# An adaptive-layernorm block on one core: another order in the prologue, the last unit and the end, and other slots for the feed-forward rows

## What is computed

```python
mod = (silu(c) @ wmod).reshape(2, 6, 1, 512)        # sa, ca, ga, sb, cb, gb
ga, gb = sign(g) * max(|g|, 0.25)                   # for both gates
h = layernorm(x) * (1 + ca) + sa
q, k, v = rope(h @ wq), rope(h @ wk), h @ wv
att = softmax(causal(q @ k.T / sqrt(128)))
x = x + ga * ((att @ v) @ wo)
h = layernorm(x) * (1 + cb) + sb
x1, x2 = split(h @ w12.T + b12)
out = x + gb * ((silu(x1) * x2) @ w3.T + b3)
```

## Time and profile before

| | us |
|---|---|
| median of three runs | 795.87 |
| the profiled execution | 795.66 |
| its span, first to last instruction | 793.9 |
| PE busy in it | 765.9 (96%) |
| DVE busy | 604.0 (76%) |
| POOL busy | 567.8 (72%) |
| ACT busy | 507.3 (64%) |

### The profile page before, as it was taken

One profiled execution on the slowest core, in us unless ns is written; L12 is line 12 of the kernel. 1 busy time (PEld: TensorE's weight loads), 2 busy tenths in 40 slices (PEclk: granted clock), 3 DMA queues, 4 the chain that ended last, 5 costly groups with the idle time before them and its releaser, 6 DMA issues.

```text
span 793.9 us, 11522 instructions
## 1 busy us (share of the span) xinstructions
PE 765.9 (96%) x3526; PEld 623.4 (79%) x3526; DVE 604.0 (76%) x1296; ACT 507.3 (64%) x1201; POOL 567.8 (72%) x384
## 2 busy tenths in 40 slices
PE   7999999999999999999999999999999998889997
PEld 2755788887888788887888888888888877667885
DVE  5777878777877787778778786868787788459685
ACT  2466775776676766786677666767677765865331
POOL 2545885879587957795779677898768998447453
PEclk9999999999999999999999999999999999999999
DMA  9625646874867576867776767866677855989011
GB/s 314 232 66 143 204 132 186 193 248 117 238 154 234 157 218 154 219 185 199 182 212 190 192 186 189 251 158 211 145 228 188 280 146 170 272 264 248 1 54 53
DMA packets 189781, 147.13 MB, mean 185 GB/s; under 512 B 60564, under 2 KB 166164, under 8 KB 187672
## 3 DMA queue, kind: packets, MB, share of 16 engines
q1 hardware_dynamic: 189304, 146.33, 65.1%
q10 hardware_dynamic: 416, 0.07, 0.0%
HBM read 91.82 MB, written 54.53 MB: 184 GB/s over the span
## 4 chain that ended last, share of the span: by engine, by line
PE 50%; POOL 22%; DVE 11%; ACT 10%; issue 4%; DMA 3%; SPq 1%; DVEq 0%; ACTq 0%; POOLq 0%
PE q_bank L511 12%; PE out_bank L599 11%; POOL pT_lo L1412 7%; PE o_bank L576 7%; PE x_bank L511 7%; PE s_bank L511 5%; POOL rope_tmp L1438 4%; ACT probs L1185 3%; POOL qT L1412 3%; POOL wo_lo_sb L1412 3%; ACT probs L1193 2%; POOL wq_lo_sb L1412 2%; PE s_bank L798 1%; PE s_bank L785 1%; DVE x_y L1134 1%
## 5 line engine op out<-in xcount | busy, mean ns | idle before, releaser
L1412 POOL TENSOR_TENSOR pT_lo<-pT_raw,pT_hi 128x1024 fp32r<-128x1024 f32 (+1 forms) x96 | 194.2, 2038 | 60.1 <-ACT pT_hi L1162 60.1
L1185 ACT ACTIVATE probs<-probs,neg_max 128x32 f32<-128x32 f32 (+15 forms) x256 | 130.6, 512 | 144.8 <-DVE neg_max L860 144.8
L1412 POOL TENSOR_TENSOR qT<-rope_tmp,qT 128x512 fp32r<-128x512 f32 x64 | 83.7, 1308 | 85.4 <-ACT qT L1162 85.4
L878 DVE STREAM_TRANSPOSE turned<-probs 128x512 f32<-128x512 f32 (+1 forms) x64 | 96.7, 1511 | 36.3 <-DMA spread_dram<-turned 28.3
L1438 POOL TENSOR_TENSOR rope_tmp<-rope_tmp 128x512 f32<-128x512 f32 x80 | 110.4, 1388 | 13.2 <-DVE rope_tmp L825 9.4
L1193 ACT ACTIVATE probs<-probs,row_inv 128x32 f32<-128x32 f32 (+15 forms) x256 | 111.9, 508 | 1.8 <-DVE row_inv L868 1.8
L511 PE MATMUL s_bank<-k_both,qT 128*128 128x416 f32 (+11 forms) x576 | 100.6, 324 | 2.0 <-DVE neg_max L860 2.0
L511 PE MATMUL q_bank<-hT_hi,wq_hi_sb 128*128 128x512 f32 x244 | 97.2, 399 | 5.1 <-DVE rope_tmp L825 5.1
L860 DVE CUSTOM_DVE_ANT_0 probs<-s_bank,mask_sb 128x416 f32<-128x416 f32 (+2 forms) x192 | 87.0, 501 | 15.9 <-PE s_bank L511 15.7
L511 PEld LDWEIGHTS s_bank<-k_both,qT 128*128 128x128 f32 x576 | 90.4, 191 | 9.9 <-DVE neg_max L860 2.6
L599 PE MATMUL out_bank<-wo_hi_sb,attn_hi 128*128 128x512 f32 x248 | 97.0, 391 | 1.2 <-DVE attn_lo L882 1.2
(11 more groups left out here) (267 smaller groups left out, 1673.2 us busy)
## 6 DMA issues: line engine op xcount, KB each, us to landing
spread_dram<-turned SPq DMA_DIRECT2D x64, 256.0 KB, 3.8
pT_raw<-spread_dram SPq DMA_DIRECT2D x16, 1024.0 KB, 5.8
spread_dram<-turned SPq DMA_DIRECT2D x64, 192.0 KB, 4.0
pT_raw<-spread_dram SPq DMA_DIRECT2D x16, 768.0 KB, 4.9
wq_raw<-in_L_attn_wq_dram SPq DMA_DIRECT2D x36, 256.0 KB, 4.2
wo_raw<-in_L_attn_wo_dram SPq DMA_DIRECT2D x9, 1024.0 KB, 5.4
spread_dram<-turned SPq DMA_DIRECT2D x64, 128.0 KB, 4.4
pT_raw<-spread_dram SPq DMA_DIRECT2D x16, 512.0 KB, 5.5
```

What stands on the lines that cost most here:

```text
L878: nc.vector.transpose(dst, src).then_inc(blocks_turned, 1)
L1185: nc.scalar.activation(rows, rows, ACT.Exp, bias=neg_max[:, par, t:t + 1], scale=-1.0, accum_out=row_sum[:, par, t:t + 1]).then_inc(exp_do ...
L1412: nc.gpsimd.tensor_tensor(dst, src, hi.bitcast(f32), ALU.subtract).then_inc(done, 1)
```

## The change

The change has four parts, which the diff shows in this order of places: the slots of the feed-forward rows and the place of their stores (SP); the prologue on PE, DVE, ACT and POOL; slot 3 of the last group and the last unit on PE, DVE, ACT and POOL; the end on PE.

- **Feed-forward rows.** `F_SLOTS` becomes 6, 9, 13, ..., 49: the second slot of each unit (r = 1), 6 for the first block. The store is the first thing in SP's slot (for most blocks r = 3, where wq, wv and wo of the next group are loaded), no longer behind the weight loads.
- **Prologue.** POOL waits for the four normalisations before `wk_low` and the first two `wq_low`, for the low parts of h before the other two, and for `norm_ready` 2 before `wv_low`; its sums and low parts then go in pairs. DVE does the second batch's statistics and norm chain ahead of all first rotations. ACT normalises the second batch before the first high part, and mixes the others with `modulate_x` otherwise. On PE `modulation_rows(3)` and `project_v(0)` change places, with other banks for modulation rows 3 and 4.
- **Last unit.** PE's order becomes scores(4), project_out(0) into q_bank, attend(1), scores(5), attend(2), project_out(1), scores(6), attend(3), turn_x1(0, (0, 1)), project_out(2), turn_x1(0, (2, 3)), scores(7), project_out(3), up(0, 0), attend(4), up(0, 1). `norm_x1(0)` goes from ACT to DVE. ACT's exponents(4) and exponents(5) come ahead of what stood before them, and maxima, low parts and adds on DVE and join_x and probs_low on POOL are reordered to match.
- **End.** The last two parts of `down(1)` are done first for rows 0 and 1, then for rows 2 and 3 together.

The diff, with most of its unchanged lines left out:

```diff
--- before.py
+++ after.py
@@ -38,7 +38,7 @@
...
 F_ROWS = 3 * KC
-F_SLOTS = [TT * (u + 2) - 1 for u in range(F_ROWS)]
+F_SLOTS = [TT + 2] + [TT * (u + 1) + 1 for u in range(1, F_ROWS)]
@@ -219,7 +219,7 @@
         MODS, TURNED = [0, 1, 3, 4, 5, 2], [0, 1, 3, 4]
-        mod_banks = [q_bank, out_bank, out_bank, q_bank, out_bank, x_bank]
+        mod_banks = [q_bank, out_bank, out_bank, s_banks[3], q_bank, x_bank]
         mod_row = [rope_tmp[0:B, 0, 0, :], rope_tmp[0:B, 0, 1, :], f_raw[0:B, :], f_raw[0:B, :], f_blocks[0:B, :], f_blocks[0:B, :]]
@@ -415,6 +415,8 @@
...
                     v = m // TT + 2
+                    if f_row_at(g, s - 2) is not None:
+                        store_f_rows(f_row_at(g, s - 2))
                     if f_row_at(g, s + 1) is not None:
@@ -448,8 +450,6 @@
...
                             load_gate(1, b)
-                    if f_row_at(g, s - 2) is not None:
-                        store_f_rows(f_row_at(g, s - 2))
                     if not (first and s == 0):
@@ -605,9 +605,9 @@
...
                         turn_rows(4)
+                        pe.wait_ge(roped, 5)
                         project_q(out_bank[:, :], 1, 0, h_lo[1])
@@ -629,36 +629,36 @@
...
                         project_v(batch_of(v))
-                    if s == 3 and last:
-                        project_out(g, s - 4)
                     if first and s == 3:
...
                         attend(g, s - 3)
-                    if s != 3 and not (first and s < 4):
+                    if (s != 3 or last) and not (first and s < 4):
                         project_out(g, s - 4)
...
                 scores(g, 4)
-                project_out(g, 0)
+                project_out(g, 0, dst=q_bank, added=-1)
                 attend(g, 1)
...
                 attend(g, 2)
+                project_out(g, 1)
+                scores(g, 6)
+                attend(g, 3)
                 pe.wait_ge(v_turned, B * KV)
+                need(pe, wo_added, SLOTS, g, 1)
                 turn_x1(0, (0, 1))
-                project_out(g, 1)
+                project_out(g, 2)
                 turn_x1(0, (2, 3))
-                scores(g, 6)
-                up(0, 0)
-                attend(g, 3)
-                project_out(g, 2)
...
                 project_out(g, 3)
+                up(0, 0)
                 attend(g, 4)
@@ -677,6 +677,9 @@
...
                         pe.wait_ge(h_ready[0], k + 1)
+                    if b == 1 and k == KC - 1:
+                        pe.wait_ge(mod_rows_copied, 3)
                     for i in range(TT):
@@ -727,9 +730,7 @@
...
             project_q(out_bank[:, :], 0, 1)
-            pe.wait_ge(wv_lo, 1)
-            pe.wait_ge(roped, 1)
-            project_v(0)
+            modulation_rows(3)
             pe.wait_ge(roped, 2)
@@ -738,9 +739,9 @@
...
             turn_x(1, range(KC))
+            pe.wait_ge(wv_lo, 1)
+            project_v(0)
             pe.wait_ge(roped, 4)
-            modulation_rows(3)
-            pe.wait_ge(roped, 5)
             modulation_rows(4)
@@ -786,13 +787,13 @@
...
-            def down(b, parts):
+            def down(b, parts, rows=range(TT)):
                 for ms in parts:
...
                         pe.wait_ge(x4_made, 3)
-                    for i in range(TT):
+                    for i in rows:
                         for m in ms:
@@ -807,7 +808,10 @@
...
                 up(1, m)
-            down(1, ([0, 1], [2], [3]))
+            down(1, ([0, 1],))
+            down(1, ([2],), range(2))
+            down(1, ([3],), range(2))
+            down(1, ([2, 3],), range(2, TT))
@@ -908,8 +912,6 @@
...
                     r = s % TT
-                    if last and s == 3:
-                        add_x1(2)
                     maxima(g, s)
@@ -921,17 +923,18 @@
...
                     if last and s == 3:
-                        x1_stats(0)
+                        add_x1(2)
+                        attn_low(g, 0)
                     invert(g, s)
...
                     if last and s == 3:
-                        x1_stats(1)
-                        x1_stats(2)
+                        for n in range(2):
+                            x1_stats(n)
                         add_x1(3)
-                        attn_low(g, 0)
-                        x1_stats(3)
+                        for n in range(2, TT):
+                            x1_stats(n)
                     else:
@@ -954,25 +957,29 @@
...
                 maxima(g, 4)
+                add_out(g, 0, src=q_bank)
+                invert(g, 4)
+                attn_low(g, 1)
                 norm_scale(0, B + 1)
-                attn_low(g, 1)
-                add_out(g, 0)
-                invert(g, 4)
+                maxima(g, 5)
+                attn_low(g, 2)
+                norm_x1(0)
                 turn_blocks(g, 4)
-                attn_low(g, 2)
-                maxima(g, 5)
-                for k in range(KC):
+                v_low(g, 1, 2)
+                add_out(g, 1)
+                invert(g, 5)
+                maxima(g, 6)
+                for k in range(2):
                     h2_low(0, k)
-                invert(g, 5)
-                add_out(g, 1)
-                v_low(g, 1, 2)
+                attn_low(g, 3)
+                add_out(g, 2)
                 turn_blocks(g, 5)
-                attn_low(g, 3)
-                maxima(g, 6)
-                add_out(g, 2)
+                for k in range(2, KC):
+                    h2_low(0, k)
                 invert(g, 6)
@@ -1001,6 +1008,13 @@
...
+            def norm_x1(b):
+                dve.wait_ge(norm_ready, B + b + 1)
+                dve.wait_ge(rope_lo, ROPE_GROUP * KV)
+                for w in range(TT * b, TT * (b + 1)):
+                    nc.vector.tensor_scalar(xn2[:, w % TT, :], acc[:, w, :], moments[:, w, 0:1], rstd[:, w, :],
+                                            ALU.subtract, ALU.mult).then_inc(x1_normed, 1)
@@ -1080,16 +1094,13 @@
...
-            dve.wait_ge(tables_in, 32)
-            first_rotation(0)
             dve.wait_ge(x_in[2], 16)
...
                 nc.vector.bn_stats(stats[:, w, :], acc[:, w, :]).then_inc(stats_made, 1)
-            first_rotation(1)
             norm_scale(1, 2)
-            first_rotation(2)
-            first_rotation(3)
-            first_rotation(4)
+            dve.wait_ge(tables_in, 32)
+            for n in range(ROPE_FIRST - 1):
+                first_rotation(n)
             for k in range(KC):
@@ -1237,10 +1248,7 @@
...
                 act.wait_ge(norm_ready, B + b + 1)
-                if b == 0:
-                    act.wait_ge(rope_lo, ROPE_GROUP * KV)
-                if b == 1:
-                    act.wait_ge(h2_turned, KC)
+                act.wait_ge(h2_turned, KC)
                 for w in range(TT * b, TT * (b + 1)):
@@ -1250,6 +1258,7 @@
...
                         q_high(g, s - 1)
+                        attn_high(g, 0)
                     exponents(g, s)
@@ -1264,10 +1273,10 @@
...
                     if last and s == 3:
-                        attn_high(g, 0)
+                        probs_high(g, s - 2)
                     if not (first and s == 0):
                         normalise(g, s)
-                    if not (first and s < 2):
+                    if not (first and s < 2) and not (last and s == 3):
                         probs_high(g, s - 2)
@@ -1286,19 +1295,18 @@
...
                 probs_high(g, 2)
+                exponents(g, 4)
                 attn_high(g, 1)
-                norm_x1(0)
-                exponents(g, 4)
                 normalise(g, 4)
                 attn_high(g, 2)
+                probs_high(g, 3)
+                v_high(g, 1, 2)
+                exponents(g, 5)
                 modulate_x1(0, (0, 1))
+                normalise(g, 5)
+                attn_high(g, 3)
                 modulate_x1(0, (2, 3))
-                probs_high(g, 3)
-                exponents(g, 5)
-                normalise(g, 5)
-                v_high(g, 1, 2)
-                attn_high(g, 3)
@@ -1353,20 +1361,20 @@
...
             wv_high(0)
-            rotated_high(0, 0, kT[0][0][:, :])
-            rotated_high(0, 1, qT[0][0][:, :, 0, :])
             act.wait_ge(norm_ready, 2)
...
                                      scale=rstd[:, w, :]).then_inc(x_normed[1], 1)
-            rotated_high(0, 2, qT[0][0][:, :, 1, :])
+            rotated_high(0, 0, kT[0][0][:, :])
+            copy_rows(3)
+            for h in range(2):
+                rotated_high(0, 1 + h, qT[0][0][:, :, h, :])
             modulate_x(1, 0)
+            rotated_high(0, 3, qT[0][0][:, :, 2, :])
             modulate_x(1, 1)
-            rotated_high(0, 3, qT[0][0][:, :, 2, :])
             modulate_x(1, 2)
+            rotated_high(0, 4, qT[0][0][:, :, 3, :])
             modulate_x(1, 3)
-            rotated_high(0, 4, qT[0][0][:, :, 3, :])
-            copy_rows(3)
             copy_rows(4)
@@ -1461,6 +1469,8 @@
...
                     q_low(g, s - 1)
```

(20 more changed lines are left out.)

## The result

The changed kernel is slower: median 803.24 us (800.98 to 803.93, four runs) against 795.42 us, a ratio of 1.0083 (95% interval 1.0066 to 1.0100). The profiled execution took 803.93 us with a span of 802.1, 8.2 more than the span before.

What follows compares the result with a forecast made beforehand. It took PE, busy 765.9 of 793.9 us, as the bound, so only its stands, low clock, start and end could save time. Prologue -2.4, slots +1.0, last unit -3.0, end -1.2 took 795.66 to 790.1 us, range 787 to 793.

Steps and rivals of the forecast that it cites:

- Slots: Slots 4 to 59: moving the feed-forward rows and their stores changes the time by +1.0 us, bounds -5.2 and +6.
- D: Slots: how much later the last spread transfer lands, from the slot's start, than in the kernel before; predicted 1.1 to 1.6.
- of 4.1 us about 1.1 is left ... Landing is 1.1 to 1.6 later: SP at r=3: wo waited for its buffer anyway, so the stores' 4.1 us delay wo by 1.1, the spread's landing 1.1 to 1.6.
- rival A: Slots: the spread's landing hardly moves, the five stalls go, -4.7 us instead of +1.0, total 784.4; chance 0.28.
- rival C: Slots: SP's queue at r=3 becomes the bound, stores delay the spread by up to 4.1 us, total 812.9; chance 0.08.
- 5D-5.2+0.5: Slots, rival C: the slots' change in us; at D=2.3 it equals the 6.6 that the other parts bring.
- Prologue: Start to scores(4): earlier normalisations and POOL's shorter wait bring -2.4 us, bounds -4.3 and -1.0.
- Last unit: Last unit: earlier scores, maxima and exponents bring attend(5) and DVE's chain forward, -3.0 us, bounds -1 and -5.
- turn_blocks(5) comes about 692.4: Last unit, DVE: this transpose, begun at 695.67 before, comes at 692.4 to 693.2, so its spreads are issued earlier.
- Rival B: Last unit gives nothing, as DVE's norm beside POOL makes maxima(5) slide by ACT's gain; total 793.1; chance 0.15.
- End: After PE's last matmul: one product and one sum remain for the last row, -1.2 us, bounds -0.4 and -1.6.

Runs made afterwards that it cites:

- e1: Changed kernel with the feed-forward rows' slots and store place as before; prologue, last unit and end stay changed: 793.02 us, ratio 0.9967.
- e2: Kernel before with only the feed-forward rows' slots and the place of their stores changed: 808.80 us, ratio 1.0150.
- the square: Changed kernel with eight or two stores per row: eight with 128 B pieces 803.2 us, 2 KB 797.1; two with 128 B 793.3, 2 KB 789.0.
- e3: Changed kernel with the eight stores in slots r=3 behind the loads of wq, wv and wo: 812.38 us, ratio 1.0207.
- e9: Changed kernel with two stores for a row instead of eight, in pieces of 128 bytes, weights permuted: 793.27 us, ratio 0.9972.
- e4: Changed kernel with the eight stores in pieces of 2 KB instead of 128 bytes, weights permuted: 797.14 us, ratio 1.0017.
- e10: e7 with the rows split at r=2, stored at r=0 of the next unit, and loaded in the turn's slot: 785.15 us, ratio 0.9864.
- e5: e1 with the rows at r=2 of each unit, split at r=3 and stored at r=0: 792.71 us, ratio 0.9955.
- e11: Kernel before with only the prologue changed: 794.92 us, ratio 0.9984.
- e7: e1 with the last unit reordered: normalise(5) and turn_blocks(5) earlier, w12 blocks 1 and 2 loaded behind the spreads: 790.44 us, ratio 0.9930.
- e8: Kernel before with only the end changed: 794.86 us, ratio 0.9978.
- e6: e4 with each part of a row stored by one DMA of 256 KB in place of four of 64 KB: 788.98 us, ratio 0.9906.

## Why the prediction was wrong

**Slots: the term that failed**, +11.6 for +1.0. The step was "of 4.1 us about 1.1 is left ... Landing is 1.1 to 1.6 later". It counted the issues on SP and let wo's own wait for its buffer absorb three of the four. The issue of wo did come only 1.9 us late. What the step left out is that wq's and wv's half megabyte had been moved in that wait (landed at 416.70 and 417.43). The stores took the time, with the engines 70% busy and at 134 GB/s, and the half megabyte was moved afterwards, ahead of wo, pT_raw and the spread. wo landed 4.7 us late and D was 3.5 us. A queue that waits at its head while its engines work is no slack.

The stand was not where the prediction had it either. It put it at the q product of slot 38, behind DVE's transpose; those stands all but went (5.1 to 1.0 us), which it had named as the sign of rival A. In the unit of slot 36, 2.4 of the 3.1 us are lost in slot 36, where PE waits 1.11 us for wo's high and 0.53 for its low part. A wait for wo was no term of the sum. e1 and e2 show that the rows and their stores make the loss, and the square that the delay shrinks with fewer and larger stores. How much of the loss is wo's landing and how much the spread's was not separated: with wo in time, e3 lost 9 us more.

So the outcome is rival C, slower by SP's queue at r=3, which had been given 0.08, and only in part by its arithmetic. Its 5D-5.2+0.5 gives 12.8 for the 11.6 measured, which is luck: it takes slot 36's D for all. The five units have D of 2.1, 2.9, 3.9, 3.5 and 3.2, for which it gives 10.5, and they lost 8.2; the units of slots 48 and 52 lost 3.4, where it has 0.5. And the units of slots 16, 24, 32 and 40, behind stores without weight loads, lost nothing, though their spreads landed 2.2 to 3.5 us later; C gave such units 2.4 of slack.

The Trainium skill, "DMA: Bandwidth & Descriptors", section "Specifications", says that transfers under 512 B do not reach line rate, which the prediction set beside rival C. The traces agree: 143 GB/s with the engines 91% busy where only such packets run (e9), 273 GB/s at 88% in e4. The piece size alone is worth 6 us of the kernel with eight stores and 4 with two. It was not the larger part: six fewer issues are worth 10 and 8 us (803.2 to 793.3, 797.1 to 789.0).

**Prologue**, -1.5 for -2.4. The rows that answer to the earlier trace rows, of the changed kernel's timeline, and the window of slots 0 and 1:

```profile
13.25 1.91 DVE L1081 TENSOR_SCALAR acc<-acc,moments,rstd 128x512 f32<-128x512 f32 x4
15.30 1.97 PE L684 MATMUL s_bank<-ident,acc 128*128 128x128 f32 x16
...
27.07 0.69 DVE L827 TENSOR_TENSOR rope_tmp<-x_bank,cos_sb 128x512 f32<-128x512 f32 x1
...
47.04 0.27 PE L555 MATMUL s_bank<-k_both,qT 128*128 128x64 f32 x1 [1.21 <-POOL qT L1420]
48.56 0.62 DVE L854 TENSOR_TENSOR probs<-s_bank,mask_sb 128x32 f32<-128x32 f32 x4
...
84.36 0.30 PE L555 MATMUL s_bank<-k_both,qT 128*128 128x64 f32 x1 [0.85 <-POOL qT L1420]
```

```profile
47.00:60.00 13.00, 12.96 (x60) 10.91 (x61) 8.90 (x30) 3.77 (x14) 3.79 (x3) 0.87 0.38 105
```

The normalisations end at 15.16 for 15.0, k's rotation begins at 27.07 for 26.5, scores(0) at 47.04 for 45.7, the maxima at 48.56 for 47.7: each step is right in kind and the gain a little smaller. The granted clock in 47 to 60 is 0.87, where it was 1.00 before: part of that window runs at 1.2 GHz. In e10 it is 1.00, scores(0) start at 47.13, and scores(4) come at 83.96, 1.9 us earlier than before. Of the ten traces with the new prologue, four (changed kernel, e1, e5, e11) have 0.87 there and scores(4) at 84.17 to 84.83; six have 1.00 and scores(4) at 83.53 to 84.23. So about half a us of the shortfall goes with the clock.

**Last unit**, -0.5 for -3.0. What the prediction derived for the maxima came true and more: maxima(5) start 6.8 us earlier against slot 59. It failed at "turn_blocks(5) comes about 692.4", which took the exponents for the last obstacle. Against slot 59 that transpose came 1.6 us earlier than before and not 3.3 to 2.5, the first issue of its spread 1.2 earlier, its landing 0.5, and PE's end 0.5. The changed kernel's ACT, DVE and SP:

```profile
697.65 0.78 ACT L1388 ACTIVATE wq_raw<-q_bank,mod,one_plus 128x512 f32<-128x512 f32 x1 [2.20 <-PE q_bank L763]
...
700.03 1.19 ACT L1204 ACTIVATE probs<-probs,row_inv 128x416 f32<-128x416 f32 x2
...
704.15 2.30 DVE L882 STREAM_TRANSPOSE turned<-probs 128x2048 f32<-128x2048 f32 x1
704.24 1.77 SPq L404 DMA_DIRECT2D hT_hi<-f_dram  x1
706.04 0.74 SPq L404 DMA_DIRECT2D hT_lo<-f_dram  x1
706.88 3.51 SPq L342 DMA_DIRECT2D spread_dram<-turned  x4
```

The exponents end at 695.4. ACT then waits 2.2 us for PE's transposes of x1, whose modulation the new order puts ahead of normalise(5), and the normalisation begins at 700.03. DVE does two low parts, attn_low(3) and an add before the transpose. SP's w12 loads end at 706.78, when the transpose does. So there were three obstacles in a row, and e7 took them away together; which of the three bound alone was not tried. Rival B gave the right number by the wrong mechanism: its "maxima(5) slides by as much as ACT won" is not seen. DVE's norm took 1.91 us for four, with POOL idle until 691.82; v_lo just behind it, beside POOL's pT_lo, took 1.93 us, where it was 0.89 before. The rule of the Trainium skill, "SBUF — State Buffer", section "Who interferes with whom" (one of the two blocks while the other has the port), found no case in the norm and agrees in kind with v_lo.

**End**, -1.3 for -1.2: right, in the trace and in e8.

## What to carry to other kernels

Before a transfer is moved to a place where the queue "waits anyway", look at what the DMA engines do in that wait: bytes in flight there are work that comes later, ahead of everything that follows. Issue cost counts per DMA, and it grew here behind large transfers and with small pieces; put many small stores where the queue waits for a landing that nothing else can hasten (e10). Here fewer of them were worth more than larger pieces. When an order is changed to start a chain earlier, follow the chain through every engine and queue to its last link, as the gain ends at the first that was not moved with it.

## What the runs showed of the hardware

- The issue of one store of 64 KB on SP took 0.44 to 0.53 us where SP went straight on (2.10 and 2.17 for four), but 2.87 and 3.33 for four behind a load of 1 MB in e3, and 4.57 for four behind a spread in e10. One store of 256 KB was issued in 0.43 us with pieces of 2 KB (e6); with pieces of 128 bytes the first took 0.43 and the second behind it 2.20 (e9).
- Where the queue moved only packets under 512 bytes it reached 143 GB/s with 91% of the engines' time (e9). In the stretch of the eight stores' issue it was 134 GB/s and 70% with pieces of 128 bytes, 273 GB/s and 88% with pieces of 2 KB, other transfers included.
- In slots 0 and 1 the granted clock was 0.87 over 13 us in the changed kernel (0.57 from 50 to 53) and 1.00 in e10, with the same program there and a start of scores(0) that differs by 0.09 us. What decides it stays open.
